# Indirect transfers without a bound on the index, with spare rows for the rows that go nowhere

## The chip, the cores and the metric

The kernel runs on one core of a Trainium2 chip. The metric is the device time in microseconds (us) of one execution; lower is better.

## The reference

A small vision model on 128 images of 2 x 104 x 104 numbers. Each image is cut into 169 patches of 8 x 8 over five shifted copies, normalised, and projected to 128 numbers, which gives N = 21,632 tokens. Two layers follow; each adds its result to the tokens. The last step is a mixture of experts, and the change lies there:

```
h = h + _L1_attn_ref(_layernorm(h, axis=-1))
h = h + _L1_ffn_ref(_layernorm(h, axis=-1), router_w, bias, shared..., w_gate, w_up, w_down)

# in _L1_ffn_ref: E = 64 experts, D = 128, F = 64, K = 6 choices, C = 4056 places for each expert
topk_p, topk_i = jax.lax.top_k(router_probs, K)
...
slot = pos - group_starts
valid = slot < C
...
expert_in = jnp.zeros((E, C + 1, D), x.dtype).at[se, safe_slot].set(x_flat[st])
...
expert_out = jnp.einsum('ecf,edf->ecd', jax.nn.silu(hg) * hu, w_down)
...
sparse = jax.ops.segment_sum(fg[:, None] * expert_out.reshape(-1, D), dst, num_segments=N + 1)[:N]
return shared_out + sparse.reshape(B, S, D)
```

Each token goes to its six best experts. An expert takes 4056 of them at most; a choice beyond that is dropped.

## The kernel before

**Stages.** `front` computes the patch projection and the first attention for 43 groups of four positions. `back` begins with a loop in which the first layer's feed-forward part and the second layer's attention (64 pairs of images, the "b" parts) are interleaved with the routing (43 groups of TG = 4 tiles of 128 tokens, the "r" parts); `braid` writes that order out, three pair places to two routing groups. Then tables are computed of which expert owns which tile of 128 rows, and the experts run over NQ = 270 groups of four tiles (`pipeline` and `weave`). At last the six results of each token are summed (`add_up`, 43 groups). 32 of those sums are woven into the late expert groups, 11 follow them.

**The scatter.** The table `xed` in HBM holds, for each expert, CR = 4224 rows of XW = 148 numbers (592 bytes: the token, its six gates and its six goals); ZR = 64 x 4224 is the first row after them, where 128 rows of zeros stand. For each routing group VectorE computes, in `place`, where each of a token's six copies goes (`idxs`, 128 x 24 indices). Four `xr` buffers take turns. On GpSimd, `scatter` (L1078) issues 24 indirect transfers for a group, each of 128 rows of `xr`, one row from each partition, to the 128 rows that a column of `idxs` names. For a choice that an expert has no place for, `place` makes the index ZR. The transfers are given a bound of ZR - 1, and a row with an index above the bound is left out.

**The spread.** The experts read tiles of 128 rows out of `xed` (`load_rows`, L1148, on SyncE's queue). TensorE transposes and multiplies, ScalarE applies the tanh and the gate (`copy_y`, L1473), and `pick` on VectorE finds the row of `ytk` that each result belongs to (`idxy`, L1797, by adding OUTSIDE to a stored number that has OUTSIDE taken off). `spread` (L1087) issues four indirect transfers for a group, each of 128 rows of 128 numbers (512 bytes), bounded by 128 x NY - 1. A row of a tile that belongs to no token of that expert has the stored number 0, so its index is OUTSIDE = 2^20, above the bound, and it is left out. The four `yo` buffers are free again when their transfers have landed.

GpSimd has no other work in these two stages. It runs all 43 `scatter` groups and then all 270 `spread` groups, in order.

Of the kernel before, what the change touches and what calls it, by code (L numbers as in the profile page):

```python
# [45 lines left out]
XW = XD + TOPK  # L46
NY = T * TOPK
OUTSIDE = float(2 ** 20)
BIG = 1e30
HALF = (128, T - 128)  # L50

# [115 lines left out]
def build(nc, io):  # L167
    def dram(name, shape):
        return nc.dram_tensor(name, shape, F32, kind="Internal").ap()

    h1d = dram("h1d", (B, T, D))
    h3d = dram("h3d", (N, D))
    h4d = dram("h4d", (N, D))
    ytk = dram("ytk", (128 * NY, D))
    gbd = nc.dram_tensor("gbd", (18, T * D), BF16, kind="Internal").ap()
    xed = dram("xed", (ZR + 128, XW))
    out = io["out"].rearrange("b t d -> (b t) d")

    with ExitStack() as ctx:
        def sb(name, shape, dt=F32, c=ctx):  # L180
            return c.enter_context(nc.sbuf_tensor(name, shape, dt))

        def sem(name):
            return ctx.enter_context(nc.semaphore(name))

        bank = [ctx.enter_context(nc.psum_tensor(f"bank{i}", [128, 512], F32)) for i in range(4)]
        wide = [ctx.enter_context(nc.psum_tensor(f"wide{i}", [128, 1024], F32)) for i in range(2)]

        ident = sb("ident", [128, 128])
        identb = sb("identb", [128, 128], BF16)  # L190
        ones = sb("ones", [128, 128])
        onesb = sb("onesb", [128, 128], BF16)
        before = sb("before", [128, 128])
        beforeb = sb("beforeb", [128, 128], BF16)
        eps_ln = sb("eps_ln", [128, 1])
        tenth = sb("tenth", [128, 1])
        wq = sb("wq", [128, 128], BF16)
        fscale = sb("fscale", [128, 4])
        mur = sb("mur", [128, B, 2, 2])

        front(nc, io, sb, bank, wide, dict(
            ident=ident, identb=identb, ones=ones, onesb=onesb, before=before, beforeb=beforeb,
            eps_ln=eps_ln, tenth=tenth, wq=wq, fscale=fscale, mur=mur), h1d, gbd, ytk)
        back(nc, io, sb, sem, bank, wide, dict(
            ident=ident, identb=identb, ones=ones, onesb=onesb, before=before, beforeb=beforeb,
            wq=wq, fscale=fscale, mur=mur, eps_ln=eps_ln), h1d, h3d, h4d, xed, ytk, out)


def front(nc, io, sb0, bank, wide, c, h1d, gbd, ytk):
# [7 lines left out]
    with ExitStack() as ctx:  # L217
# [60 lines left out]
        qtmp = sb("qtmp", [128, D])  # L278
        qm = sb("qm", [128, D])
        zeros = sb("zeros", [128, 384])  # L280
        ytz = ytk[:, :].rearrange("(p n) d -> p (n d)", p=128)

        s_img = [sem(f"s_img{i}") for i in range(4)]
        s_zero = sem("s_zero")
# [607 lines left out]
def back(nc, io, sb0, sem, bank, wide, c, h1d, h3d, h4d, xed, ytk, out):  # L892
# [53 lines left out]
    jk = sb("jk", [128, TG, TOPK])  # L946
    token = sb("token", [128, 1])
    tokeni = sb("tokeni", [128, 1], I32)
    idxs = sb("idxs", [128, 4, TG, TOPK], I32)
    uptob = sb("uptob", [128, 128], BF16)  # L950

# [102 lines left out]
    with nc.Block() as block:  # L1054
        @block.gpsimd
        def _(p):
# [6 lines left out]
            p.memset(col[:, :], 0.0)  # L1063
            p.iota(eiota[:, :], [[0, 2]], base=0, channel_multiplier=1)
            p.iota(tokeni[:, :], [[0, 1]], base=0, channel_multiplier=NY)
            p.iota(firsti[:, :], [[CR, NE]], base=1, channel_multiplier=0)
            p.iota(iiota[:, :], [[128, M0]], base=0, channel_multiplier=0).then_inc(n["s_c"], 1)

            def scatter(g, slot, rnd):
# [6 lines left out]
                for j in range(nj):  # L1076
                    for k in range(TOPK):
                        p.indirect_dma_start(  # L1078
                            xed[:, :], bass.IndirectOffsetOnAxis(ap=idxs[:, slot, j, k:k + 1], axis=0),
                            xr[:, slot, j, :], None, bounds_check=ZR - 1, oob_is_err=False).then_inc(scat[slot], 16)  # L1080

            def spread(q, slot, rnd):
                p.wait_ge(n["idxy_r"], q + 1)
# [2 lines left out]
                for j in range(TG):  # L1086
                    p.indirect_dma_start(  # L1087
                        ytk[:, :], bass.IndirectOffsetOnAxis(ap=idxy[:, slot, j:j + 1], axis=0),
                        yo[:, slot % ES, j, :], None, bounds_check=128 * NY - 1, oob_is_err=False)\
                        .then_inc(yo_out[slot % ES], 16)  # L1090

            pipeline(p, 0, GR, [(0, scatter)], 4)
# [3 lines left out]
        def _(sp):  # L1096
# [53 lines left out]
            def load_y(g, slot, rnd, kept=False):  # L1150
                nj = tiles_of(g)
                after(sp, n["ot_r"], g - 1)
                sp.dma_start(yg[:, slot, 0:nj, :, :],
                             ytk[:, :].rearrange("(p t k) d -> p t k d", p=128, k=TOPK)[:, bass.ds(TG * g, nj), :, :])\
                    .then_inc(yg_in[slot], 16)
                if kept:
                    return
# [324 lines left out]
        def _(v):  # L1482
# [126 lines left out]
            def place(g, slot, rnd):  # L1609
# [16 lines left out]
                for j in range(nj):  # L1626
# [1 line left out]
                last.then_inc(n["dk_r"], 1)  # L1628

                v.wait_ge(n["dk_r"], g + 1)  # L1630
                v.tensor_scalar(zk[:, 0:nj, :], dk[:, 0:nj, 0:TOPK], 0.0, float(ZR + 1), ALU.is_equal, ALU.mult)\
                    .then_inc(n["zk_r"], 1)
                v.wait_ge(n["zk_r"], g + 1)
                v.scalar_tensor_tensor(idxs[:, slot, 0:nj, :], dk[:, 0:nj, 0:TOPK], -1.0, zk[:, 0:nj, :],
# [48 lines left out]
            def constants():  # L1683
# [6 lines left out]
                link(v.memset(col[C:C + 1, 8:9], float(ZR)))  # L1690
                link(v.memset(col[C:C + 1, 4:5], float(ZR)))
                link(v.tensor_copy(token[:, :], tokeni[:, :]))
                link(v.tensor_copy(jk[:, :, :].rearrange("p j k -> p (j k)"), jki[:, :]))
                link(v.tensor_copy(first1[:, :], firsti[:, :]))

# [84 lines left out]
            def pick(q, slot, rnd):  # L1780
# [13 lines left out]
                v.wait_ge(n["gi_r"], q + 1)  # L1794
                if not isinstance(q, int) or q >= EI:
                    v.wait_ge(yo_out[slot % ES], 16 * TG * (2 * rnd + slot // ES - 1))
                v.tensor_scalar(idxy[:, slot, :], gi[:, slot, :, 1], OUTSIDE, None, ALU.add).then_inc(n["idxy_r"], 1)  # L1797

            def act_e(q, slot, rnd):
                half = slot % 2  # L1800
# [117 lines left out]
```

## Time and profile before

| | |
|---|---|
| median of 3 runs | 3563.5 us (3563.09 to 3573.16) |
| span of the profiled execution | 4731.8 us |
| the profiled execution's own time beside its span | none is given; the span stands for it |
| busy: TensorE, VectorE, ScalarE, GpSimd | 59%, 48%, 33%, 53% of the span |
| packets and bytes of GpSimd's queue | 83,232 packets, 126.60 MB |
| mean granted clock of TensorE | 0.660 |

The execution under the profiler took a third longer than the plain runs. Durations of single instructions are read from the profile, and a sum of them has to be set against both numbers. A line of a view gives the source line, the engine, the operation with the tiles it writes and reads, how often it occurs, and times; "idle before" is the time in which its engine waited ahead of it.

### The profile page before, as it was taken

How to read it: one execution, taken by the hardware profiler on the slowest of the kernel's cores; microseconds unless marked ns; L12 is line 12 of the kernel's file. 1: busy time of each engine (PE TensorE's matmuls, PEld its weight loads, DVE VectorE, ACT ScalarE, POOL GpSimd, SP SyncE). 2: the span in 40 equal slices, each digit the busy share in tenths (PEclk: the TensorE clock that was granted, in tenths of full speed). 3: DMA queues.
4: the chain of work that ended last, by engine and by line, in shares of the span. 5: the costliest groups of instructions: out<-in, count | busy, mean ns of one | idle time of the engine just before them, and what ended most of it. 6: DMA issues, size and time to landing. Idle time of an engine off the chain costs nothing. (4 is left out here: it accounts for less than half of the span.)

```text
span 4731.8 us, 65133 instructions
## 1 busy us (share of the span) xinstructions
PE 2774.4 (59%) x14071; PEld 2094.8 (44%) x14072; DVE 2253.7 (48%) x7746; ACT 1579.8 (33%) x4281; POOL 2487.3 (53%) x2516
## 2 busy tenths in 40 slices
PE   6888856545454544545455256676666666666661
PEld 5777733322232322323223145565555555555550
DVE  6999964544354444444444233333333333336555
ACT  6888743322232222222232112222222222222220
POOL 5777604545445454454544645555555555556661
PEclk8999955555555555555555567766767777777775
DMA  8777611212111121111111123333232322236667
GB/s 287 243 247 245 215 37 55 67 61 65 64 62 62 56 68 51 57 55 51 55 49 52 45 68 90 92 93 90 82 82 82 83 81 75 79 97 219 210 216 251
DMA packets 401860, 501.33 MB, mean 106 GB/s; under 512 B 70904, under 2 KB 334193, under 8 KB 390482
## 3 DMA queue, kind: packets, MB, share of 16 engines
q1 hardware_dynamic: 318514, 373.60, 26.0%
q0 software_dynamic: 83232, 126.60, 8.2%
q14 instruction: 90, 0.74, 0.1%
q8 instruction: 24, 0.39, 0.0%
HBM read 257.02 MB, written 264.08 MB: 110 GB/s over the span
## 5 line engine op out<-in xcount | busy, mean ns | idle before, releaser
L1078 POOL DMA_INDIRECT xed<-xr,idxs x1014 | 996.8, 983 | 1106.0 <-DVE xr L1655 701.0
L1087 POOL DMA_INDIRECT ytk<-yo,idxy x1080 | 1067.3, 988 | 835.1 <-issue 796.5
L1334 PE MATMUL wide<-wdt,hT 64*128 x2160 | 457.7, 374 | 576.6 <-DVE hT L1813 554.3
L1334 PEld LDWEIGHTS wide<-wdt,hT 64*128 64x128 f32 x2160 | 391.7, 269 | 627.4 <-issue 619.8
L1804 DVE SCALAR_TENSOR_TENSOR ae<-the,bank 128x256 f32<-128x256 f32 x270 | 113.7, 421 | 851.3 <-ACT the L1464 795.1
L1473 ACT ACTIVATE yo<-wide,gi 128x128 f32<-128x128 f32 x1080 | 307.2, 370 | 327.5 <-issue 180.3
L1316 PE MATMUL bank<-wgu,xeT 128*128 x2160 | 401.4, 346 | 23.9 <-issue 16.5
L1316 PEld LDWEIGHTS bank<-wgu,xeT 128*128 128x128 f32 x2160 | 379.2, 263 | 36.1 <-issue 34.4
L1238 PE MATMUL bank<-xnT 128*128 128x169 f32 (+1 forms) x512 | 205.2, 529 | 296.1 <-issue 263.4
L1249 PE MATMUL wide<-xn,e 128*128 128x128 f32 (+3 forms) x1024 | 279.9, 398 | 154.2 <-ACT e L1401 144.5
L1464 ACT ACTIVATE the<-bank 128x256 f32<-128x256 f32 x270 | 107.5, 398 | 649.2 <-remote 553.0
L589 POOL TENSOR_TENSOR weff<-w,gam 128x384 f32<-128x384 f32 x338 | 305.5, 936 | 10.5 <-DMA tokb<-in_tokb 9.0
L1813 DVE COPY hT<-wide 64x512 f32<-64x512 f32 x270 | 183.4, 679 | 260.4 <-issue 144.1
L1458 ACT ACTIVATE xeT<-bank 128x512 f32<-128x512 f32 x270 | 164.4, 609 | 419.2 <-remote 214.4
L1249 PEld LDWEIGHTS wide<-xn,e 128*128 128x128 f32 (+3 forms) x1024 | 158.9, 205 | 273.1 <-ACT e L1401 158.3
L1306 PE MATMUL bank<-ident,xin 128*128 128x128 f32 x1080 | 235.6, 359 | 64.3 <-DMA xin<-xed 62.2
L1238 PEld LDWEIGHTS bank<-xnT 128*128 128x128 f32 (+1 forms) x512 | 91.2, 235 | 382.9 <-issue 373.9
L1598 DVE SCALAR_TENSOR_TENSOR sa<-th,wide 128x512 f32<-128x512 f32 (+1 forms) x43 | 29.2, 679 | 437.3 <-issue 305.8
L1325 PE MATMUL wide<-ident,hh 128*64 128x128 f32 x1080 | 232.4, 354 | 0.0
L1306 PEld LDWEIGHTS bank<-ident,xin 128*128 128x128 f32 x1080 | 186.3, 190 | 77.9 <-issue 44.5
L621 PE MATMUL bank<-weff,xs 128*128 128x128 f32 x1690 | 199.3, 278 | 1.0 <-POOL weff L589 1.0
L621 PEld LDWEIGHTS bank<-weff,xs 128*128 128x128 f32 x1690 | 195.3, 195 | 2.6 <-issue 2.6
(318 smaller groups left out, 5110.6 us busy)
## 6 DMA issues: line engine op xcount, KB each, us to landing
xin<-xed SPq DMA_DIRECT2D x1080, 74.0 KB
ytk<-zeros SPq DMA_DIRECT2D x42, 1536.0 KB, 9.6
yg<-ytk SPq DMA_DIRECT2D x42, 1536.0 KB
xs<-in_xcol SPq DMA_DIRECT2D x42, 1280.0 KB, 6.7
ytk<-yo,idxy POOLq DMA_INDIRECT x1080
xed<-xr,idxs POOLq DMA_INDIRECT x1014
H<-in_ximg SPq DMA_DIRECT2D x4, 2704.0 KB, 22.3
h1d<-H SPq DMA_DIRECT2D x42, 256.0 KB, 9.5
```

Source lines behind the costliest of these rows:

```text
L589: ins = p.tensor_tensor(weff[:, slot, j, k0:k1, :], w5[:, k0:k1, :], gam[:, bass.ds(TG * g + j, 1), k0:k1].rearrange("p o c -> p (o c)").u ...
L621: pe.matmul(psY[slot][:, j * D:(j + 1) * D], xs[:, slot, j, k, :], weff[:, slot, j, k, :], start=(j == 0 and k == 0), stop=False)
L1078: p.indirect_dma_start(xed[:, :], bass.IndirectOffsetOnAxis(ap=idxs[:, slot, j, k:k + 1], axis=0), xr[:, slot, j, :], None, bounds_check=Z ...
L1087: p.indirect_dma_start(ytk[:, :], bass.IndirectOffsetOnAxis(ap=idxy[:, slot, j:j + 1], axis=0), yo[:, slot % ES, j, :], None, bounds_check ...
L1238: last = pe.matmul(dst, xnT[:, i, 128 * h:128 * h + m], xnT[:, i, 0:T], start=True, stop=True)
L1249: last = pe.matmul(pP[0:m, 256 * i + D * h:256 * i + D * h + D], e[0:m2, i, 128 * h:128 * h + m], xn[0:m2, slot, 2 * i + h2_, :], start=(h ...
L1306: last = pe.transpose(eT_[slot % 2][:, j * 128:(j + 1) * 128], xin[:, slot, j, 0:D], ident[:, :])
L1316: last = pe.matmul(eG[slot % 2][:, j * 128:(j + 1) * 128], xeT[:, slot % 2, j, :], wgu[:, bass.ds(e, 1), :].rearrange("p o f -> p (o f)"), ...
L1325: last = pe.transpose(eH[slot % 2][0:F, j * 128:(j + 1) * 128], hh[:, slot % 2, j, :], ident[:, :])
L1334: last = pe.matmul(eO[slot % 2][:, j * D:(j + 1) * D], hT[:, slot % 2, j, :], wdt[:, bass.ds(e, 1), :].rearrange("p o f -> p (o f)"), star ...
L1473: last = a.activation(yo[:, slot % ES, j, :], eO[slot % 2][:, j * D:(j + 1) * D], ACT.Copy, scale=gi[:, slot, j, 0:1])
L1813: v.tensor_copy(hT[:, slot % 2, :, :].rearrange("p j d -> p (j d)"), eH[slot % 2][0:F, :])\
```

## The change

Both kinds of indirect transfer lose their bound. So that every index is a real row, `xed` gets 96 x 128 spare rows behind its rows of zeros and `ytk` gets 32 x 128 behind its own. Two more index tables (`spilli`, one number for each transfer of four scatter groups and of eight spread groups, in each partition) are made on GpSimd at the start and turned into float numbers on VectorE. In `place`, `zk` becomes (dk == 0) x the spare row instead of (dk == 0) x (ZR + 1), so that a dropped copy goes to a spare row that belongs to this partition, this transfer and this buffer slot. In `pick`, `idxy` becomes the smaller of (number + OUTSIDE) and the spare row.

```
 SPILL_X = 4 * TG * TOPK
 SPILL_Y = 8 * TG
-    ytk = dram("ytk", (128 * NY, D))
+    ytk = dram("ytk", (128 * (NY + SPILL_Y), D))
-    xed = dram("xed", (ZR + 128, XW))
+    xed = dram("xed", (ZR + 128 * (1 + SPILL_X), XW))
...
+            p.iota(spilli[:, 0:SPILL_X], [[128, SPILL_X]], base=ZR + 129, channel_multiplier=1)
+            p.iota(spilli[:, SPILL_X:SPILL_X + SPILL_Y], [[128, SPILL_Y]], base=128 * NY, channel_multiplier=1)
...
                         p.indirect_dma_start(
                             xed[:, :], bass.IndirectOffsetOnAxis(ap=idxs[:, slot, j, k:k + 1], axis=0),
-                            xr[:, slot, j, :], None, bounds_check=ZR - 1, oob_is_err=False).then_inc(scat[slot], 16)
+                            xr[:, slot, j, :], None).then_inc(scat[slot], 16)
...
                     p.indirect_dma_start(
                         ytk[:, :], bass.IndirectOffsetOnAxis(ap=idxy[:, slot, j:j + 1], axis=0),
-                        yo[:, slot % ES, j, :], None, bounds_check=128 * NY - 1, oob_is_err=False)\
+                        yo[:, slot % ES, j, :], None)\
                         .then_inc(yo_out[slot % ES], 16)
...
-                v.tensor_scalar(zk[:, 0:nj, :], dk[:, 0:nj, 0:TOPK], 0.0, float(ZR + 1), ALU.is_equal, ALU.mult)\
+                v.scalar_tensor_tensor(zk[:, 0:nj, :], dk[:, 0:nj, 0:TOPK], 0.0, spill_x[:, slot, 0:nj, :],
+                                       ALU.is_equal, ALU.mult)\
                     .then_inc(n["zk_r"], 1)
...
+                link(v.tensor_copy(spill[:, :], spilli[:, :]))
...
-                v.tensor_scalar(idxy[:, slot, :], gi[:, slot, :, 1], OUTSIDE, None, ALU.add).then_inc(n["idxy_r"], 1)
+                v.scalar_tensor_tensor(idxy[:, slot, :], gi[:, slot, :, 1], OUTSIDE, spill_y[:, slot, :], ALU.add, ALU.min).then_inc(n["idxy_r"], 1)
```

The zeroing of `ytk` in `front` and the loads of the sums address the first 128 x NY rows, as before.

## Rows read from the trace of the kernel before

**Rows 1.** Busy time by stage: engines in order, clock, DMA share, GB/s.

```profile
0.00:750.00 750.00, 594.80 (x3702) 465.90 (x3703) 612.05 (x1716) 522.14 (x1081) 423.18 (x422) 0.87 0.60 203
750.00:2745.00 1995.00, 961.49 (x3877) 551.83 (x3877) 875.55 (x3825) 524.76 (x1580) 996.76 (x1014) 0.53 0.18 58
2783.00:4647.00 1864.00, 1198.09 (x6411) 1065.07 (x6409) 694.89 (x2063) 527.38 (x1608) 1067.09 (x1080) 0.72 0.39 111
4647.00:4731.80 84.80, 0.00 (x0) 0.00 (x0) 56.11 (x102) 0.00 (x0) 0.00 (x0) 0.50 0.88 311
```

**Rows 2.** GpSimd's groups: out<-in, count, busy and mean, idle before.

```profile
L1087 POOL DMA_INDIRECT ytk<-yo,idxy x1080 | 1067.3, 988 | 835.1 <-issue 796.5 <-ACT yo L1473 38.6
L1078 POOL DMA_INDIRECT xed<-xr,idxs x1014 | 996.8, 983 | 1106.0 <-DVE xr L1655 701.0 <-issue 405.0
```

**Rows 3.** GpSimd in order of time: start, duration, idle before.

```profile
1513.70 0.97 POOL L1078 DMA_INDIRECT xed<-xr,idxs  x1 [0.30 <-issue]
1514.98 0.97 POOL L1078 DMA_INDIRECT xed<-xr,idxs  x1 [0.30 <-issue]
...
2743.48 0.97 POOL L1078 DMA_INDIRECT xed<-xr,idxs  x1 [0.30 <-issue]
2782.76 0.97 POOL L1087 DMA_INDIRECT ytk<-yo,idxy  x1 [38.30 <-ACT yo L1473]
2784.03 0.97 POOL L1087 DMA_INDIRECT ytk<-yo,idxy  x1 [0.30 <-issue]
2785.31 0.97 POOL L1087 DMA_INDIRECT ytk<-yo,idxy  x1 [0.30 <-issue]
...
4574.86 1.36 POOL L1087 DMA_INDIRECT ytk<-yo,idxy  x1 [0.30 <-issue]
```

**Rows 4.** Lines L1078 and L1087: min, median, max ns, first and last start.

```profile
L1078 POOL DMA_INDIRECT xed<-xr,idxs x1014: 967/972/1692, 750.3 to 2743.5; - x169
L1087 POOL DMA_INDIRECT ytk<-yo,idxy x1080: 969/972/2198, 2782.8 to 4646.0; - x180
L1087 POOLq MOVE  x1080: 29/29/29, 2782.0 to 4640.1; - x180
```

**Rows 5.** Line L1078 from 1512 to 1516.8 us: the queue runs ahead.

```profile
L1078 POOLq MOVE  x9: 29/29/38, 1512.2 to 1516.5; - x9
L1078 POOL DMA_INDIRECT xed<-xr,idxs x4: 973/974/975, 1512.4 to 1516.3; - x4
```

**Rows 6.** SyncE's queue on L1148, 3508 to 3516 us, then 3517 to 3521.

```profile
L1148 SPq MOVE xin<-xed x4: 3/359/702, 3510.9 to 3515.3; - x4
```
```profile
L1148 SPq MOVE xin<-xed x4: 6/29/29, 3517.7 to 3519.3; - x4
```

**Rows 7.** GpSimd's DMA queue: whole run; 2900 to 4000; 4300 to 4500; 4500 to 4646.

```profile
q0 software_dynamic: 83232, 126.60, 8.2%
```
```profile
q0 software_dynamic: 20320, 40.94, 11.0%
```
```profile
q0 software_dynamic: 3772, 3.53, 5.5%
```
```profile
q0 software_dynamic: 2680, 0.05, 1.4%
```

**Rows 8.** Line L1087 from 2900 to 4000 us, and from 4500 to 4646.

```profile
L1087 POOL DMA_INDIRECT ytk<-yo,idxy x635: 969/972/1012, 2899.9 to 3999.2; - x159
```
```profile
L1087 POOL DMA_INDIRECT ytk<-yo,idxy x87: 969/972/2198, 4500.1 to 4646.0; - x87
```

**Rows 9.** GpSimd's index ramps at the start of the second part.

```profile
L1066 POOL IOTA firsti<- 128x64 int32 x1 | 0.2, 178 | 0.0
L1065 POOL IOTA tokeni<- 128x1 int32 x1 | 0.1, 123 | 0.0
```

**Rows 10.** VectorE on L1631, L1634 and L1797: min, median, max ns.

```profile
L1631 DVE TENSOR_SCALAR zk<-dk x43: 173/178/179, 747.1 to 2711.3; 128x24 f32<-128x24 f32 x42, 128x6 f32<-128x6 f32 x1
```
```profile
L1634 DVE SCALAR_TENSOR_TENSOR idxs<-dk,zk x43: 166/182/184, 747.3 to 2711.5; 128x24 int32<-128x24 f32 x42, 128x6 int32<-128x6 f32 x1
```
```profile
L1797 DVE TENSOR_SCALAR idxy<-gi x270: 170/171/458, 2770.5 to 4620.7; 128x4 int32<-128x4 f32 x135
```

**Rows 11.** Busy time from 4300 to 4500 us.

```profile
4300.00:4500.00 200.00, 122.40 (x691) 109.56 (x689) 117.57 (x305) 57.81 (x175) 121.09 (x116) 0.74 0.68 213
```

More of the change, by code:

```diff
@@ L48 @@
 OUTSIDE = float(2 ** 20)
+SPILL_X = 4 * TG * TOPK
+SPILL_Y = 8 * TG
 BIG = 1e30
@@ L280, in front @@
         zeros = sb("zeros", [128, 384])
-        ytz = ytk[:, :].rearrange("(p n) d -> p (n d)", p=128)
+        ytz = ytk[0:128 * NY, :].rearrange("(p n) d -> p (n d)", p=128)
         s_img = [sem(f"s_img{i}") for i in range(4)]
@@ L948, in back @@
     tokeni = sb("tokeni", [128, 1], I32)
+    spilli = sb("spilli", [128, SPILL_X + SPILL_Y], I32)
+    spill = sb("spill", [128, SPILL_X + SPILL_Y])
+    spill_x = spill[:, 0:SPILL_X].rearrange("p (s j k) -> p s j k", s=4, j=TG)
+    spill_y = spill[:, SPILL_X:SPILL_X + SPILL_Y].rearrange("p (s j) -> p s j", j=TG)
     idxs = sb("idxs", [128, 4, TG, TOPK], I32)
@@ L1153, in load_y @@
                 sp.dma_start(yg[:, slot, 0:nj, :, :],
-                             ytk[:, :].rearrange("(p t k) d -> p t k d", p=128, k=TOPK)[:, bass.ds(TG * g, nj), :, :])\
+                             ytk[0:128 * NY, :].rearrange("(p t k) d -> p t k d", p=128, k=TOPK)[:, bass.ds(TG * g, nj), :, :])\
                     .then_inc(yg_in[slot], 16)
```

## Prediction

> **What bounds the kernel now.** I read the table of stages first [rows 1]. From 750 us to 2745 us GpSimd issues its 1014 scatters, and from 2783 us to 4647 us its 1080 spreads; in neither stage is any engine full, by this profile: TensorE is busy 961 of 1995 us and 1198 of 1864 us, GpSimd 997 and 1067. The groups of GpSimd [rows 2] say the same: 1106 us and 835 us idle. So read plainly, the profile says that GpSimd is half idle and that its speed is worth little.
>
> The profiled span is 4731.8 us, though, and the plain runs take 3563.5 us. Two rows show that the profiler itself holds the engines up. A register move on SyncE's queue takes 29 ns as a rule, and up to 702 ns from 3508 to 3516 us, where it depends on nothing [rows 6]; such stretches come again and again in the two late stages. The waits around them (GpSimd for VectorE, GpSimd for ScalarE) can't be taken as waits of the plain run.
>
> What stays the same everywhere is GpSimd's own pace. Within a group the transfers follow each other at 1513.70, 1514.98 us and at 2782.76, 2784.03, 2785.31 us [rows 3]: 1.278 us from start to start for a scatter, 1.275 for a spread, of which 0.97 are busy and 0.30 between. Now the sum as if GpSimd never waited: 750.3 us to the first scatter [rows 4], 1014 x 1.278 = 1295.9, 38.3 from the last scatter to the first spread [rows 3], 1080 x 1.275 = 1377.0, and 84.8 for the sums behind the last spread [rows 1]. Together 3546 us, which is 17 us or 0.5% under the median of the plain runs, and 1186 us under the profiled span. I take from this that in a plain run the indirect transfers are end to end on the path, in both stages: 2094 of them, 2673 us of 3563. Had the plain run's first 750 us been much shorter, there would be room for waits; nothing in the first stage is slack enough for that to be large (TensorE busy 595 and VectorE 612 of 750).
>
> **The change, part by part.**
>
> *The register move.* Each transfer has a move of 29 ns on GpSimd's queue [rows 4], presumably the bound, and it goes. From 1512 to 1516.8 us there are 9 moves and 4 transfers [rows 5]: the queue is some five instructions ahead of the engine, at 4.3/8 = 0.54 us each against 1.278. So the move is hidden behind the transfer before it and is worth 0. Were that cover gone (a pace under 0.54 us), it would be 0.03 x 2094 = 61 us.
>
> *The test in the transfer.* This is the whole question, and the trace has no transfer without a bound. What it does show: the test is made, since a row left out moves almost no bytes but still has its packet (2680 packets with 0.05 MB at the end, 32 for each transfer as in the full stretch, 20320/635) [rows 7]. And its cost doesn't hang on its result: the median is 972 ns where nearly every row is written and 972 ns where none is [rows 8]. So the test is not a branch that a left-out row takes; it is the same work for each of the 128 indices, or none that shows. Bounds: from below it costs 0 (it may be done beside other work of the same transfer); from above all that is busy can't be the test, and I put it at three steps for each index (compare, choose the address, choose the length). The nearest price of a step for each element on GpSimd is that of the index ramps: 178 ns for 64 elements and 123 for one [rows 9], 0.87 ns per element. One step over 128 indices is 0.112 us, three are 0.335 us. I take one step: the 972 ns for 128 indices are 7.6 ns for each, room for some nine steps of 0.87 ns in which a whole descriptor is made twice over (read and write side), and a compare with a choice can lie partly beside them. 2094 x 0.112 = 234 us.
>
> The Trainium skill (GPSIMD Engine Reference, section 3.1) puts a data-dependent branch at about 12 cycles for each element. An estimate by it, at that page's 1.2 GHz, is 1.28 us for 128 indices, more than the whole busy time of a transfer, and rows 8 show no dependence on the data; so the rule doesn't describe this test.
>
> *More bytes.* Rows left out are now written in full. Full size would be 1014 x 128 x 592 = 76.8 MB and 1080 x 128 x 512 = 70.8 MB, 147.6 in all; 126.6 were moved [rows 7], so 21 MB are added. In the scatter stage the DMA engines are 18% busy and in the spread stage 39% [rows 1]. They hide it. The exception is the end, where the sums are loaded beside the spreads: from 4300 to 4646 us 203 transfers moved 3.6 MB, and will move 13.3; the DMA engines are 68% busy there [rows 11]. A transfer met by such a load takes 1.36 us instead of 0.97 [rows 3], so this end may cost a few us; I put 3. If the cover were gone, it is the rival below.
>
> *VectorE.* `zk` gets a tensor operand: L1634 is that same kind of instruction on the same shape and takes 182 ns against 178 [rows 10]. `idxy` likewise, 171 to some 180 ns. 43 x 4 and 270 x 10 ns, behind an engine that is 44% and 37% busy: 0. They lie ahead of `scatter` and `spread`, whose indices are ready one group early once GpSimd is the slow one. The two ramps and the copy at the start, about 0.2 us each [rows 9], lie in the 750 us and cost below 1 us.
>
> *What is late next.* TensorE needs 961.5/1014 = 0.948 us for each scatter and 1198.1/1080 = 1.109 us for each spread, at granted clocks of 0.53 and 0.72 [rows 1]. With a pace of 1.166 and 1.163 us GpSimd stays the slower one, by little in the second stage. The first, middle and last pieces (750 + 38 + 85 us) don't change.
>
> Sum: 3563.5 - 234 + 3 = 3332 us. Between the likeliest case's own ends (half a step, a step and a half) lie 3215 and 3450 us.
>
> **The rivals.**
>
> *No change: the test costs nothing that shows.* For it: the duration is the same for full and for left-out rows [rows 8], and the same within 10 ns for rows of 592 and 512 bytes [rows 4]; it may be set by something other than the work for each index, such as writing the descriptors out or telling 16 engines. Against it: nothing, since no row separates the two. Time: 3563.5 + 0 to 3, so 3560 to 3570 us.
>
> The Trainium skill (DMA: Bandwidth & Descriptors, "Anatomy of one DMA") calls descriptor generation a small, variable part of which many can be made before the cost shows; by that the bound's removal would leave 3563 us. The constant 972 ns agrees with it, the 1.28 us pace that fills 2673 us speaks against "small".
>
> *More: the test is three steps.* The pace would fall by 0.335 us to 0.943, below TensorE's 0.948 and 1.109; TensorE then bounds both stages: 1014 x (1.278 - 0.948) = 335 us and 1080 x (1.275 - 1.109) = 179 us, 514 in all, 3050 us. Less if VectorE's and ScalarE's links in each group don't follow, and more if TensorE's clock is granted higher when it waits less.
>
> *Slower: the added bytes at the end.* If the test costs nothing and the DMA engines are the bound from 4300 us on, the 9.7 MB added there are paid at the rate of the last stretch, 311 GB/s [rows 1]: 31 us, 3595 us. It decides only once those engines are full; at 68% now, and with gaps, they have room for 9.7 MB in 346 us (28 GB/s beside 213) [rows 11]. A part of it, over 11 us, already makes the kernel slower.
>
> *The change doesn't do what it says.* Without a bound given the same code may still compare with some largest value; that is the first rival's time, and within its chance.
>
> **How the numbers follow.** A measurement of this kernel tells a difference from none at about 0.3%, 11 us. About one step (3215 to 3550 us): 0.42. Clearly more, down to 3050 us or below: 0.20. No change: 0.25. Slower: 0.13. So faster 0.62, same 0.25, slower 0.13. The predicted time is 3332 us. The range for 8 in 10 leaves out the slower case and what lies below the three-step case: 3050 to 3572 us. The likeliest case alone has 3215 to 3450 us.
>
> **What would show it.** In the profile after, the start-to-start time of transfers within a group says everything: about 1.165 us if I am right, 1.275 for no change, 0.95 or less for the larger case; the 0.30 us between two transfers should stay. No move should stand on L1078 and L1087. GpSimd's queue should show 83,232 packets and about 147.6 MB. `zk` and `idxy` should take about 180 ns. The span may fall by another amount than the plain time, since the profiler's own stops fill part of it. The prediction is wrong if the pace doesn't move, or if it moves and the time doesn't follow by 2094 times the difference: then my reading that GpSimd is on the path throughout was wrong.

## The result: 17 us faster, 0.5%

The changed kernel takes 3554.61 us (median of 7 runs, 3537.44 to 3558.07), the kernel before, on the same chip, 3568.24 (7 runs, 3559.98 to 3573.16). The ratio is 0.9952, with a 95% interval of 0.9936 to 0.9968: by the ratio 17 us faster, between 11 and 23 (the medians themselves differ by 13.6). The forecast was 3332 us, which is 232 faster than the 3563.5 it set out from. The direction was right, and the size was out by more than ten times.

The chips that the runs fell on differ: the kernel before takes about 3565 us on some of them and 4660 to 4760 us on others, in plain runs as under the profiler, and by its span of 4731.8 us its profile ahead of the prediction was taken on a slow one. The profile after comes from a fast one, so it stands beside a second profile of before (the first experiment) and not beside [rows 1].

The profile after, engines first (busy time, share of the span, instructions; PE is TensorE, PEld its weight loads, DVE VectorE, ACT ScalarE, POOL GpSimd), and GpSimd's DMA queue (packets, MB, share of 16 engines):

```profile
span 3553.5 us, 63042 instructions
PE 2577.1 (73%) x14071; PEld 1901.0 (53%) x14072; DVE 2226.5 (63%) x7747; ACT 1564.2 (44%) x4281; POOL 2478.6 (70%) x2518
q0 software_dynamic: 83232, 147.75, 12.1%
```

Busy time by stage (columns as in [rows 1]): before the first scatter, scatters, spreads, the rest.

```profile
0.00:757.50 757.50, 594.81 (x3702) 464.95 (x3703) 615.96 (x1718) 522.50 (x1081) 423.57 (x424) 0.86 0.60 201
757.50:2098.50 1341.00, 942.67 (x4028) 542.61 (x4029) 891.58 (x3886) 535.65 (x1610) 1001.56 (x1014) 0.59 0.31 95
2098.50:3481.00 1382.50, 1039.62 (x6344) 893.47 (x6342) 671.32 (x2061) 506.06 (x1591) 1053.44 (x1080) 0.83 0.54 160
3481.00:3553.50 72.50, 0.00 (x0) 0.00 (x0) 47.66 (x87) 0.00 (x0) 0.00 (x0) 0.50 0.85 302
```

The two transfers by source line (min/median/max ns, first and last start), which answer to [rows 4]; no move stands beside them now:

```profile
L1086 POOL DMA_INDIRECT xed<-xr,idxs x1014: 957/963/1526, 757.5 to 2097.2; - x169
L1095 POOL DMA_INDIRECT ytk<-yo,idxy x1080: 955/962/2194, 2098.5 to 3479.8; - x180
```

And the groups, busy and idle before (for [rows 2]), with that of ScalarE that makes `yo`. An idle time that ended in "issue" is one in which the engine waited for nothing that the profile shows:

```profile
L1086 POOL DMA_INDIRECT xed<-xr,idxs x1014 | 1001.6, 988 | 447.5 <-issue 302.5
L1095 POOL DMA_INDIRECT ytk<-yo,idxy x1080 | 1053.4, 975 | 329.1 <-issue 325.1
L1481 ACT ACTIVATE yo<-wide,gi 128x128 f32<-128x128 f32 x1080 | 308.7, 368 | 853.4 <-DMA ytk<-yo,idxy 822.1
```

The spreads' idle time is 329.1 us, and 1080 times the median gap of 0.305 us is 329.4; the longest gap in the stage is 0.32 us. So GpSimd waits for nobody there. ScalarE, on the other hand, waits 822 us for spreads to land. The busy share of GpSimd in the two stages, 75% and 76%, hides this, since the gap of 0.30 us between two transfers is not counted. At the change of stages the spreads follow in the same beat, where [rows 3] had a gap of 38 us:

```profile
2097.24 0.96 POOL L1086 DMA_INDIRECT xed<-xr,idxs  x1 [0.31 <-issue]
2098.51 0.96 POOL L1095 DMA_INDIRECT ytk<-yo,idxy  x1 [0.30 <-ACT yo L1481]
2099.77 0.96 POOL L1095 DMA_INDIRECT ytk<-yo,idxy  x1 [0.30 <-issue]
```

The pace (median from start to start within a group) is 1.268 us for a scatter and 1.266 for a spread, against 1.279 and 1.277 in before's second profile. That is 11 ns less, where 112 were forecast.

### The profile page after: what moved, and what is told of

The parts are those of the page before. It is cut to its first block and busy times, and to the rows that moved or that the text cites. A ratio compares the mean times of both kernels' runs of the same rounds, so it can differ in the third digit from the quotient of the medians.

```text
span 3553.5 us, 63042 instructions
## 1 busy us (share of the span) xinstructions
PE 2577.1 (73%) x14071; PEld 1901.0 (53%) x14072; DVE 2226.5 (63%) x7747; ACT 1564.2 (44%) x4281; POOL 2478.6 (70%) x2518
## 3 DMA queue, kind: packets, MB, share of 16 engines
q0 software_dynamic: 83232, 147.75, 12.1%
## 5 line engine op out<-in xcount | busy, mean ns | idle before, releaser
L1095 POOL DMA_INDIRECT ytk<-yo,idxy x1080 | 1053.4, 975 | 329.1 <-issue 325.1
L1342 PE MATMUL wide<-wdt,hT 64*128 x2160 | 373.2, 323 | 164.4 <-DVE hT L1823 162.7
L1324 PE MATMUL bank<-wgu,xeT 128*128 x2160 | 367.8, 323 | 155.4 <-ACT xeT L1466 154.1
L1324 PEld LDWEIGHTS bank<-wgu,xeT 128*128 128x128 f32 x2160 | 326.8, 231 | 200.6 <-issue 199.9
L1342 PEld LDWEIGHTS wide<-wdt,hT 64*128 64x128 f32 x2160 | 313.9, 220 | 215.6 <-issue 212.6
L1257 PE MATMUL wide<-xn,e 128*128 128x128 f32 (+3 forms) x1024 | 249.6, 364 | 43.2 <-ACT e L1409 43.2
L1257 PEld LDWEIGHTS wide<-xn,e 128*128 128x128 f32 (+3 forms) x1024 | 142.6, 185 | 148.6 <-issue 72.5
L602 POOL TENSOR_TENSOR big<-big,scb 128x1024 f32<-128x1024 f32 (+1 forms) x43 | 106.0, 2464 | 159.5 <-ACT big L735 159.5
L1314 PE MATMUL bank<-ident,xin 128*128 128x128 f32 x1080 | 202.5, 320 | 8.6 <-DMA xin<-xed 8.6
L1333 PE MATMUL wide<-ident,hh 128*64 128x128 f32 x1080 | 206.4, 323 | 0.0
L1314 PEld LDWEIGHTS bank<-ident,xin 128*128 128x128 f32 x1080 | 161.2, 169 | 13.5 <-issue 8.3
L1442 ACT ACTIVATE x4T<-wide 128x512 f32<-128x512 f32 (+1 forms) x43 | 25.4, 590 | 315.6 <-PE wide L1265 315.6
```

Of the source, the lines that this page charges most:

```text
L1095: p.indirect_dma_start(ytk[:, :], bass.IndirectOffsetOnAxis(ap=idxy[:, slot, j:j + 1], axis=0), yo[:, slot % ES, j, :], None)\
L1257: last = pe.matmul(pP[0:m, 256 * i + D * h:256 * i + D * h + D], e[0:m2, i, 128 * h:128 * h + m], xn[0:m2, slot, 2 * i + h2_, :], start=(h ...
L1314: last = pe.transpose(eT_[slot % 2][:, j * 128:(j + 1) * 128], xin[:, slot, j, 0:D], ident[:, :])
L1324: last = pe.matmul(eG[slot % 2][:, j * 128:(j + 1) * 128], xeT[:, slot % 2, j, :], wgu[:, bass.ds(e, 1), :].rearrange("p o f -> p (o f)"), ...
L1333: last = pe.transpose(eH[slot % 2][0:F, j * 128:(j + 1) * 128], hh[:, slot % 2, j, :], ident[:, :])
L1342: last = pe.matmul(eO[slot % 2][:, j * D:(j + 1) * D], hT[:, slot % 2, j, :], wdt[:, bass.ds(e, 1), :].rearrange("p o f -> p (o f)"), star ...
```

## The experiments

The kernels with a bound again are cut to those lines; all else in them is the changed kernel. Paces are medians from start to start within a group.

**The kernel before, profiled on a fast chip** (no edit).

> The kernel before, unchanged, for a second profile. Theory A (GpSimd's transfers are end to end on the path in a plain run, and the profile of before was slowed by the profiler): the span is near 3560 us, the scatters and spreads follow each other at 1.277 and 1.275 us with hardly a wait between groups, and about 17 us more are spent in the two stages than after the change. Theory B (the waits of rows 2 are real and the plain run is fast for another reason): idle time of several hundred us ahead of the transfers again. The ratio to the kernel before is 1.000.

3566.67 us beside 3567.2, ratio 1.000 [0.9988, 1.0012]. Its two lines, its register moves, and SyncE's queue on L1148; then busy time in the two stages:

```profile
L1078 POOL DMA_INDIRECT xed<-xr,idxs x1014: 967/974/1480, 748.9 to 2089.1; - x169
L1087 POOL DMA_INDIRECT ytk<-yo,idxy x1080: 971/972/1977, 2090.4 to 3485.4; - x180
L1087 POOLq MOVE  x1080: 29/29/29, 2080.6 to 3468.4; - x180
L1148 SPq MOVE xin<-xed x1080: 29/29/38, 2064.3 to 3431.4; - x180
```
```profile
748.90:2090.40 1341.50, 939.24 (x4031) 540.55 (x4032) 897.54 (x3887) 535.90 (x1611) 1004.30 (x1014) 0.60 0.29 88
2090.40:3486.70 1396.30, 1030.02 (x6340) 883.57 (x6338) 680.41 (x2062) 505.67 (x1590) 1067.39 (x1080) 0.84 0.52 151
```

The scatter stage takes 1341.5 us and not 1995, the spread stage 1396 and not 1864, with nearly the same time for each transfer, 974 and 972 ns, as in [rows 4]. The moves on L1148, up to 702 ns in [rows 6], take 38 ns at most. The span is 3557.6 us, and the execution under the profiler took 3559.50, no more than the plain ones. So the prediction was wrong that the profiler held the engines up. The long moves come with the slow chips: every profile from one has 236 to 341 register moves of over 100 ns, on all queues together, and no profile from a fast one has any. (Each chip was used at one time only, so whether it is the chip itself or its condition then is not shown.) Apart from 28 us of waits in the scatter stage, in 13 gaps, GpSimd is end to end, and in the spread stage there is no gap over 0.32 us: this much the prediction had right, from a profile in which it could not be seen.

**A bound that no index meets.** The spare rows are written as in the change.

```
-   xr[:, slot, j, :], None)
+   xr[:, slot, j, :], None, bounds_check=ZR + 128 * (1 + SPILL_X) - 1, oob_is_err=False)
-   yo[:, slot % ES, j, :], None)
+   yo[:, slot % ES, j, :], None, bounds_check=128 * (NY + SPILL_Y) - 1, oob_is_err=False)
```

> The changed kernel with its spare rows and index work, and with a bound that no index exceeds. Theory A (the bound itself costs some 10 ns for each transfer, hidden nowhere): the pace goes back from 1.268 and 1.266 us to 1.277 and 1.275, and the time to that of before, 3565 us, ratio 1.000. Theory B (the gain comes from the rows, since a row left out was written as a tiny packet and is now a full one): the pace and the time stay at those after the change, ratio 0.995. Theory C (the gain is that of the register move on GpSimd's queue): as A in the time, so the pace decides nothing here; the isolated transfers do.

3564.59 beside 3567.2, ratio 0.9994 [0.9981, 1.0006]: the gain is gone. The durations are those of before (paces 1.278 and 1.276 us):

```profile
L1086 POOL DMA_INDIRECT xed<-xr,idxs x1014: 967/973/1486, 750.2 to 2095.9; - x169
L1095 POOL DMA_INDIRECT ytk<-yo,idxy x1080: 971/972/1897, 2097.1 to 3490.5; - x180
```

This kernel has all of the change but the missing bound: more bytes (147.75 MB), other index arithmetic, spare rows. Together these change the time by -7 to +2 us, which is nothing clear of noise, and the bound is the gain. It comes back in the duration of the transfer; the gap between two transfers is 0.305 us with and without it.

**The bound on the scatter alone.**

```
-   xr[:, slot, j, :], None)
+   xr[:, slot, j, :], None, bounds_check=ZR - 1, oob_is_err=False)
```

> The changed kernel with the bound of before on the scatters alone (rows above it are left out again), none on the spreads. Theory A (10 ns for each transfer): 1014 x 0.010 = 10 us of the 17 to 20 us gain are gone, ratio 0.997 to 0.998; scatters at 1.277 us, spreads at 1.266. Theory B (only rows that are now written matter): the same split by rows left out, 15,000 on scatters against 24,000 on spreads, so ratio 0.997, but the pace of the scatters is 1.268.

3558.86 beside 3567.2, ratio 0.9972 [0.9958, 0.9986]: about half the gain by the medians, though the interval overlaps with that of the whole change.

```profile
L1086 POOL DMA_INDIRECT xed<-xr,idxs x1014: 967/973/1479, 757.7 to 2102.9; - x169
L1095 POOL DMA_INDIRECT ytk<-yo,idxy x1080: 954/958/1947, 2104.2 to 3481.5; - x180
```

The shorter transfer follows the bound, line by line. The unbounded spread has a pace of 1.263 us here, 13 ns under that of the bound that is never met, where the changed kernel's has 1.266. So the price of a bound in these kernels is 10 to 14 ns.

**The transfers by themselves.** A program with nothing of the model issues 48 transfers of each kind one after another, and waits for them to land between kinds (one execution). A transfer has one index in each partition, and 128, 64 or 16 partitions.

```
L50: 128 rows, bound met by none   L53: 128 rows, no bound   L56, L59: 64 rows, with and without
L62, L65: 16 rows, with and without   L68: 128 rows, all above the bound
L71, L74: rows of 2048 and 64 bytes, no bound   L77: plain transfer of 128 rows
```

> Nothing of the model is computed; GpSimd issues 48 indirect transfers of each kind with nothing beside them: 128 rows of 512 bytes with a bound and without; 64 rows with and without; 16 rows with and without; 128 rows all above the bound; rows of 2048 and of 64 bytes without; and 48 plain copies. Theory A (the bound costs a fixed 10 ns for each transfer, or less than 0.1 ns for each index): 1.275 against 1.266 us for 128 rows, and about the same difference for 64 and 16 rows if it is fixed, a half and an eighth if it is for each index. My prediction's term (0.87 ns for each index) would give 0.112, 0.056 and 0.014 us. If descriptors are made one by one, the pace falls with the number of rows; if a fixed part rules, 64 rows still take over 1 us. Rows all above the bound: as those within it. The length of a row changes nothing until the DMA engines are full.

Busy and mean ns of one, then idle before:

```profile
L50 POOL DMA_INDIRECT table<-src,idx x48 | 46.9, 977 | 15.2 <-issue 14.3 <-POOL out_of L37 0.9
L68 POOL DMA_INDIRECT table<-src,out_of x48 | 46.7, 974 | 16.6 <-issue 16.6
L71 POOL DMA_INDIRECT wide<-src,idx x48 | 46.1, 961 | 16.2 <-issue 14.3 <-DMA table<-src,out_of 1.9
L74 POOL DMA_INDIRECT narrow<-src,idx x48 | 46.0, 958 | 16.8 <-issue 14.3 <-DMA wide<-src,idx 2.5
L53 POOL DMA_INDIRECT table<-src,idx x48 | 46.0, 958 | 16.3 <-issue 14.3 <-DMA table<-src,idx 2.0
L56 POOL DMA_INDIRECT table<-src,idx x48 | 43.6, 908 | 16.4 <-issue 14.3 <-DMA table<-src,idx 2.1
L59 POOL DMA_INDIRECT table<-src,idx x48 | 43.0, 896 | 16.3 <-issue 14.3 <-DMA table<-src,idx 2.0
L62 POOL DMA_INDIRECT table<-src,idx x48 | 40.5, 843 | 16.4 <-issue 14.3 <-DMA table<-src,idx 2.1
L65 POOL DMA_INDIRECT table<-src,idx x48 | 40.2, 838 | 16.2 <-issue 14.3 <-DMA table<-src,idx 1.9
L77 POOL DMA_DIRECT2D table<-src x48 | 25.5, 540 | 1.7 <-DMA narrow<-src,idx 1.7
```

The paces are 1.277 us with a bound and 1.263 without for 128 indices, 1.212 and 1.202 for 64, 1.147 and 1.142 for 16. So without a bound an index costs (1.263 - 1.142)/112 = 1.08 ns and the transfer itself 1.142 - 16 x 0.00108 = 1.125 us. The bound costs 14, 10 and 5 ns: some 4 for the transfer and 0.08 for each index. It costs the same where every row is left out (L68, 1.277), and the length of the rows changes 3 ns at most (L71 1.266, L74 1.263). The prediction had seen the two last points in [rows 8] and [rows 4].

**One spread more, one spread less in a group of four.** The first writes a fifth time to rows of its own behind the spare ones, by a fixed list; the second leaves the fourth tile's rows out of the sum. Both change the waits on `yo_out` to five or three transfers.

```
 (more)
+   p.indirect_dma_start(ytk[:, :], bass.IndirectOffsetOnAxis(ap=extra[:, slot:slot + 1], axis=0),
+       yo[:, slot % ES, 0, :], None).then_inc(yo_out[slot % ES], 16)
 (less)
-   for j in range(TG):
+   for j in range(TG - 1):
```

> The changed kernel, and in each of the 270 spread groups a fifth indirect transfer, of 128 rows that go to spare rows of their own and that nobody reads. Theory A (GpSimd's transfers are end to end on the path): 270 x 1.266 = 342 us more, 3896 us, ratio 1.092. Theory B (the wait for TensorE or for landing would be there anyway): clearly less than 342.

> The changed kernel without the fourth transfer of each spread group, so the fourth tile of rows never reaches the sum. Theory A: up to 342 us less, 3212 us; the group then takes 3.80 us on GpSimd, and TensorE needs 1040/270 = 3.85 at its granted clock, so 3212 to 3240 us and a first sight of the next bound. Theory B: less than half of it.

These fell on a slow chip (before: 4666.2 us): 4936.35, ratio 1.0596 [1.0564, 1.0627], and 4238.19, ratio 0.9083 [0.9053, 0.9114]. On two more slow chips:

> One indirect transfer more in each spread group. On a chip at 3567 us, theory A (end to end on the path): 342 us more than after the change, 3896 us, ratio 1.092. Theory B (something else is as late as GpSimd): clearly less, as it was on the chip at 4666 us (270 us more than before).

> The fourth transfer of each spread group left out, on another chip. On a chip at 3567 us: theory A up to 342 us less than after the change, 3212 us, or 3240 if TensorE is next at 3.85 us for each group; ratio 0.90 to 0.91. The first time, on a chip at 4666 us, it was 428 us less than before.

> One indirect transfer more in each spread group. On a chip at 3567 us, theory A: 342 us more than after the change, 3896 us, ratio 1.092; theory B: clearly less, as on the chips at 4666 and 4758 us, where it was 270 and 318 us more than before.

5075.94 beside 4757.87, 1.0681 [1.0657, 1.0705]; 4258.76 beside 4662.94, 0.9139 [0.9116, 0.9162]; 4956.77 beside 4662.94, 1.0638 [1.061, 1.0666]. Each is 270 transfers, worth 342 us at 1.266. If the changed kernel is put at 0.9904 of before (below), they came to 315, 383, 364, 359 and 339 us. Even on a slow chip, then, where GpSimd waits 420 to 480 us in that stage with four spreads a group, a spread more or less costs about its full pace. The spread more was also run on a fast chip; the spread less was not, so what fewer transfers would give there has to be read from the last experiment:

> One indirect transfer more in each spread group. On a chip at 3567 us, theory A: 342 us more than after the change, 3896 us, ratio 1.092. On the three chips at 4660 to 4760 us it was 1.060 to 1.068.

3888.82 beside 3560.92, ratio 1.0926 [1.0901, 1.0952].

```profile
L1097 POOL DMA_INDIRECT ytk<-yo,idxy x1080 | 1048.6, 971 | 329.1 <-issue 327.2 <-DVE idxy L1812 1.2 <-ACT yo L1486 0.6
L1101 POOL DMA_INDIRECT ytk<-yo,extra x270 | 263.2, 975 | 82.3 <-issue 82.3
```

The changed kernel was not run beside it; its ratio gives 0.9952 x 3560.92 = 3543.8 us there, and 345 us more for 270 transfers is 1.28 us for each. The profiles say the same: from the first spread to the last it takes 1721.8 us here and 1381.3 in the changed kernel, 340 us more. That is the whole pace, with nothing hidden, so the spreads are the path. No scatter was added or taken away.

**The changed kernel, and the bound on the spread alone, on slow chips.** The edit of the second is `bounds_check=128 * NY - 1, oob_is_err=False` in `spread`.

> The changed kernel with the bound of before on the spreads alone, none on the scatters: the other half of the change. Theory A (a fixed gain of 10 to 14 ns for each transfer, all of it on the path): 10 us faster than before, ratio 0.997. Theory C (in the scatter stage the gain is given back, because VectorE's part of the next group is late and its instructions stretch transfers; there the stage took 1341 us with and without the bound): ratio 0.999 to 1.000, scatters at 1.266 us within a group and the stage still at 1341 us.

> The changed kernel once more, beside the others of this call on one chip. On a chip where the kernel before takes 3567 us: 3555 us, ratio 0.995 to 0.996, transfers at 1.268 and 1.266 us. On a chip like that of the profile of before (4666 us in plain runs too), where instructions of all queues are held for 0.7 us at a time in the late stages: theory A (only the pace counts) 20 us less, ratio 0.996; theory D (there the supply of instructions is the bound, and 2094 register moves fewer help as well): ratio 0.98 or lower.

> Bound kept on the spreads, none on the scatters, again. On a chip at 3567 us: theory A 10 us less, ratio 0.997; theory C (given back in the scatter stage) 0.999 to 1.000. The spreads follow each other at 1.276 us, not at the 1.288 of the first time, if that was the chip's doing.

The bound on the spread: 4604.0 beside 4666.2, 0.9877 [0.9855, 0.9899], and on the other chip 4729.85 beside 4757.87, 0.9929 [0.9912, 0.9947]. The change itself on that other chip: 4712.66, 0.9904 [0.9886, 0.9922], 45 us. The same kernel twice gives intervals that don't overlap, so the slow chips can't settle half a per cent. Nor does the pace account for their gains: it gives some 26 us of the 45, and nothing of the 57 and 34 of the bounded spreads, whose scatters come 9 and 12 ns sooner than in before's profile and whose spreads as much later. What else is gained there is open, and the scatter's half of the change has no time of its own on a fast chip. One row was not expected:

```profile
L1095 POOL DMA_INDIRECT ytk<-yo,idxy x1080: 981/984/3076, 2671.4 to 4494.8; - x180
```

Here a bounded spread takes 984 ns (pace 1.289 us) and not 972. The same was seen in the second of these kernels (1.288) and in the next program (L82, 1.289): in each of the three the program's first indirect transfer has no bound, and in the four programs whose first one has a bound, those with one take 972 to 974 (medians). All three ran on slow chips, but so did the profile of [rows 4], which has 972. Why is open.

**The transfers beside other engines' work.** Again 48 of each kind and nothing of the model, one execution, on a slow chip.

```
L54: alone, no bound   L58: while VectorE adds tensors of 128 x 512   L63: while VectorE adds a constant to one of 128 x 512
L68: while ScalarE copies 128 x 512   L79: an empty instruction ahead of each   L82: with bound
L73/L75: with and without a bound by turns, 24 each   L85: gathers that each wait for the one before
```

> Nothing of the model is computed; 48 indirect transfers of 128 rows of 512 bytes each time: without a bound and with nothing beside them; beside VectorE's additions of two 128x512 tiles; beside VectorE's additions of a constant to one; beside ScalarE's copies; with and without a bound in turn; with an empty instruction ahead of each; with a bound; and as gathers of which each waits for the one before. Theory A: 1.263 us alone, and again beside ScalarE and with the empty instruction if the queue hides it. Theory C (VectorE's instructions stretch transfers, which is where part of the scatter stage's gain went): 1.35 us or more beside the additions. If the register move were what costs, an instruction more ahead of each transfer would bring 1.275 us back.

```profile
L63 POOL DMA_INDIRECT table<-src,idx x48 | 58.0, 1209 | 16.4 <-issue 14.3 <-DMA table<-src,idx 2.1
L58 POOL DMA_INDIRECT table<-src,idx x48 | 54.9, 1143 | 16.4 <-issue 14.3 <-DMA table<-src,idx 2.1
L54 POOL DMA_INDIRECT table<-src,idx x48 | 46.3, 964 | 14.6 <-issue 14.3 <-POOL out_of L41 0.3
L79 POOL DMA_INDIRECT table<-src,idx x48 | 46.1, 961 | 16.3 <-issue 14.3 <-DMA table<-src,idx 2.0
L68 POOL DMA_INDIRECT table<-src,idx x48 | 46.1, 961 | 17.7 <-issue 14.3 <-DVEq L103 3.4
L82 POOL DMA_INDIRECT table<-src,idx x48 | 47.3, 985 | 16.4 <-issue 14.3 <-DMA table<-src,idx 2.1
L73 POOL DMA_INDIRECT table<-src,idx x24 | 23.9, 995 | 7.3 <-issue 7.3
L75 POOL DMA_INDIRECT table<-src,idx x24 | 23.2, 966 | 21.5 <-ACTq L112 14.5 <-issue 7.0
```

An empty instruction more on the queue costs nothing (L79, pace 1.266 as alone); that the register move costs nothing either is likely by this, and was not run by itself. In this program, whose first transfer has no bound, a bound costs more than in the last: 985 against 964 ns, and by turns 995 against 966. A gather that waits for the one before has a pace of 2.74 us (L85). VectorE's work stretches a transfer from 0.96 to 1.14 and 1.21 us, ScalarE's leaves it alone. That is far more than the bound: a single transfer that VectorE meets can lose what the missing bound gives back in about 20.

**Groups with nothing in them skipped.** Of the 270 expert groups 39 begin with a tile that holds no row of any expert (924 of 1080 spreads are left). GpSimd reads from the table of tiles whether a group is one of them, and then one plain transfer of 128 rows to spare rows takes the place of its four spreads.

```
+   row, = entries(POOL, tin, TG * q, 1, ZR)
+   with p.If(row < ZR):
        for j in range(TG): ...
+   with p.Else():
+       p.dma_start(ytk[128 * (NY + TG * slot):128 * (NY + TG * slot + 1), :],
+                   yo[:, slot % ES, 0, :]).then_inc(yo_out[slot % ES], 16 * TG)
```

> The changed kernel, where GpSimd reads from the table of tiles whether a group of four begins with an empty tile; then it issues one plain copy of 128 x 512 bytes to spare rows in place of the four indirect transfers, which carry only rows that go nowhere. By the trace of before some 148 spreads at the end carry nothing, 37 groups. Theory A: these groups go from 5.06 us to what TensorE needs, 3.85, so 45 us less, 3510 us, ratio 0.984 against the kernel before. If reading the table and branching isn't hidden behind the transfers (0.55 us of the queue for each against 1.266), each of the 270 groups grows and the gain is lost.

> Empty spread groups get one plain copy. In the first run 924 indirect spreads were left of 1080, so 39 groups were skipped. On a chip at 3567 us: 39 x (5.06 - 3.85) = 47 us less than after the change if TensorE sets the pace of the skipped groups, 3508 us, ratio 0.983; up to 39 x 4.5 = 175 us less if they pass at GpSimd's pace (0.57 us).

> Empty spread groups get one plain copy (39 groups). On a chip at 3567 us, theory A: 47 us less than after the change if TensorE sets the pace of the skipped groups, 3508 us, ratio 0.983; up to 175 us less if they pass at GpSimd's pace. On the slower chips the ratio was 0.975 and 0.976.

> Empty spread groups get one plain copy (39 groups). On a chip at 3567 us, theory A: 47 us less than after the change if TensorE sets the pace of the skipped groups, 3508 us, ratio 0.983; up to 175 us less if they pass at GpSimd's pace. On the slower chips the ratio was 0.975 to 0.977.

On slow chips 4546.08 beside 4666.2, 0.9752 [0.9727, 0.9776]; 4641.77 beside 4757.87, 0.9759 [0.9741, 0.9777]; 4564.36 beside 4662.94, 0.977 [0.9738, 0.9803]. On a fast one 3519.61 beside 3560.92, 0.988 [0.9863, 0.9897]. It beats both kernels: 41 us under before, and 24 under the changed kernel's 3543.8, a number that is itself good to some 6 us. The spreads that are left and the plain transfers, on the fast chip:

```profile
L1098 POOL DMA_INDIRECT ytk<-yo,idxy x924: 955/962/1359, 2094.6 to 3271.6; - x185
L1103 POOL DMA_DIRECT2D ytk<-yo x39: 537/540/618, 2969.7 to 3422.0; - x39
```

The plain transfers in order of time; then waits from 3270 to 3450 us (total, times, longest), and busy time near the end:

```profile
3309.84 0.54 POOL L1103 DMA_DIRECT2D ytk<-yo  x1 [4.13 <-ACT yo L1487]
3314.62 0.54 POOL L1103 DMA_DIRECT2D ytk<-yo  x1 [4.24 <-ACT yo L1487]
```
```profile
POOL ytk L1103 <- ACT yo L1487: 122.3, 33, 6.9
ACT yo L1487 <- PE wide L1348: 63.5, 32, 5.1
```
```profile
3300.00:3450.00 150.00, 91.88 (x604) 82.37 (x604) 118.91 (x297) 52.18 (x155) 14.56 (x27) 0.78 0.94 307
```

39 x 4 spreads at 1.266 are 197 us, and 24 came of them. The skipped groups lie almost all at the end, where GpSimd now waits some 4 us ahead of each for ScalarE's `yo`: a group passes in 4.3 us (median) instead of the 5.06 of four spreads, and 39 x 0.73 = 28 us is about what was found. VectorE and the DMA engines are 79% and 94% busy there; which of them sets the 4.3 us was not tested. A saving past the point where something else bounds is not paid out.

That all dropped rows go to one set of spare rows wasn't tried, since two transfers under way would then write the same rows in no order.

## Why the size was wrong and the direction right

- **The price of the test failed, and with it the forecast.** It was the step "I take one step: the 972 ns for 128 indices are 7.6 ns for each, room for some nine steps". That division assumed that a transfer's time is the sum of its indices' times. The rows for 128, 64 and 16 indices show that 1.125 of 1.263 us don't depend on the number of indices, and an index costs 1.08 ns. A test of 0.87 ns would nearly have doubled that. Measured: 14 ns alone and 11 in the kernel, about 0.1 ns an index where 0.87 was forecast. The prediction had no row for a second list length, and took the middle of its bounds instead of the lower end, to which both of its own findings pointed: the same time for rows left out [rows 8], and the same for rows of two sizes [rows 4].
- **The sum held for the spreads; the scatters gave next to nothing.** The prediction pays out 2094 times the difference in pace. With the measured 10.5 ns that is 22 us, at the edge of the interval of 11 to 23 us. Counted in the profiles from the first scatter to the end, it is 12.8 us (2808.7 to 2795.9). The spread stage gave 14 us (1396.3 to 1382.5, where the count gives 11). The scatter stage gave 0.5 (1341.5 to 1341.0, where it should give 10), and not in these two executions alone. On fast chips it took 1341.5, 1346.9 and 1346.4 us in three kernels with a bound on the scatter, and 1341.0, 1341.5 and 1346.6 in three without. What eats the gain is in part a term that the prediction doesn't have, transfers stretched beside VectorE's work. Taking those more than 15 ns over their median, 131 to 136 scatters lose 16 to 17 us in the three kernels with a bound, and 139 to 141 lose 23 to 26 us in the three without. Every one of them runs beside an instruction of VectorE (in the changed kernel 53 of the 72 scatters that meet L1517, on 128 x 512 numbers, are among them, where it is 141 of all 1014). So about 7 of the 10 us are given back each time; why the shorter transfers are stretched more is open. Waits for late rows (28 to 39 us in the six) make up the rest of the differences between these executions.
- **The reading of the profile was half wrong.** The transfers are nearly end to end in both stages, as the sum of 3546 us said; for the spreads the fifth one showed it with its 345 us, for the scatters the trace alone shows it. But that the profiler holds up the engines was a false explanation of the gap of 1170 us. The slow chips do it without a profiler. What on them stretches register moves to 0.7 us and up to 1.5, in the late stages and never in the first 740 us, is open.
- **What was costed at nothing cost nothing that shows.** The ramps and copies at the start, VectorE's longer instructions, and the 21 MB: the bound that is never met put all of them to the test together, 0.9994. The register move is still in that kernel; for it there is only the empty instruction of L79. The queue has 83,232 packets and 147.75 MB, as forecast. `zk` and `idxy` have medians of 182 and 163 ns, where about 180 were named for both:

```profile
L1639 DVE SCALAR_TENSOR_TENSOR zk<-dk,spill x43: 165/182/203, 754.4 to 2029.3; 128x24 f32<-128x24 f32 x42, 128x6 f32<-128x6 f32 x1
L1807 DVE SCALAR_TENSOR_TENSOR idxy<-gi,spill x270: 161/163/228, 2077.3 to 3446.1; 128x4 int32<-128x4 f32 x135
```

- **The rivals.** "No change" was nearest in size: 3560 to 3570 us against 3554.61. What the Trainium skill says there (DMA: Bandwidth & Descriptors, "Anatomy of one DMA": descriptor generation is a small, variable part) fits the index's share, 1.08 ns, and the bound's; it doesn't fit the 1.125 us that every indirect transfer costs GpSimd whatever the number of its indices. "More" and "slower" did not occur: the last stretch, behind the spreads, is 72.5 us after and 70.9 in before's second profile, 1.6 us more where the sum has 3.

In the profile after, the first scatter starts at 757.5 us and not at 748.9. Most of the difference arises at 57 us, far from all that was changed, in one instruction of VectorE beside GpSimd's own tensor work. After, and the kernel with the bound that is never met (first scatter at 750.2):

```profile
57.16 8.98 DVE L786 TENSOR_SCALAR xh<-H,mv,rs 128x128 f32<-128x128 f32 x1 [0.60 <-ACT rs L707]
```
```profile
57.40 3.50 DVE L786 TENSOR_SCALAR xh<-H,mv,rs 128x128 f32<-128x128 f32 x1 [0.60 <-ACT rs L707]
```

Of the 18 profiles of the whole kernel and its variants, five have it at 8.8 to 9.1 us and the first scatter at 757.5 to 758.7; the others have 4.0 us at most and 747.5 to 750.4. The kernel with one spread more is in both groups (758.0 and 749.6), and so are the changed kernel and the one with skipped groups. So it belongs to the execution and not to the change.

## What to carry to other kernels

Where one engine issues indirect transfers end to end, multiply their number by the time from start to start, and not by the busy time: here 2094 x 1.27 us are three quarters of the kernel, at a busy share that looks moderate. Almost all of that price is for the transfer and not for its indices, its bytes or its bound, so cut the number of transfers (fill the list of indices, skip the empty ones) before making each cheaper, and expect less than the count as soon as another engine is close. A gain of 10 ns a transfer can be eaten by contention that the sum doesn't have: look for stretched transfers before and after. To price a step inside an instruction, look for the same instruction in two sizes first; and set a profile's span against plain times of the same chip before explaining the gap between them.

## What the runs showed of the hardware

- An indirect transfer takes GpSimd 1.263 us from start to start for 128 indices, 1.202 for 64, 1.142 for 16; a plain one 0.53. A bound adds 14, 10 and 5 ns, and in the three programs whose first indirect transfer had no bound, 12 more for 128 indices.
- VectorE's work on 128 x 512 numbers stretches it by 0.18 to 0.25 us, ScalarE's not at all; and one VectorE instruction beside GpSimd's tensor work took 9 us in five of 18 profiles, and 4 us at most in the others.
- The same kernel takes 3565 us on some chips and 4660 to 4760 on others. The first 750 us are alike; the late stages are not.
